# A graph layer with a gated delta-rule recurrence: norms by roots on ScalarE, logits with nodes stationary, five gate tiles behind the recurrence, output tile by tile

## The reference

```python
xn = layernorm(x)
x = x + gnn(xn, W, b, edges) + linear_attention(xn)
x = x + ffn(layernorm(x))

def ffn(h):                                   # E, TOPK, H, DK, DV, D = 4, 2, 8, 64, 64, 512
    scores = softmax(h @ Wgate);  rw, sel = top_k(scores, 2);  rw /= rw.sum()
    q = l2norm(silu(h @ Wq));  k = l2norm(silu(h @ Wk));  v = silu(h @ Wv)     # per head
    beta = sigmoid(h @ Wb);    g = -exp(A_log) * softplus(h @ Wa + dt_bias)
    # for each expert, over the nodes that chose it, in order:
    S = S * exp(g_t);  delta = (v_t - k_t @ S) * beta_t;  S += outer(k_t, delta);  o_t = (q_t / 8) @ S
    core = sum over the two chosen experts of rw * o
    core = core * rsqrt(mean(core * core, per head) + 1e-5) * o_norm_weight * silu(h @ Wg)
    return core @ Wo

def l2norm(x): return x * rsqrt(sum(x * x) + 1e-6)
```

## Time and profile before

| | us |
|---|---|
| median of 3 runs (lowest to highest) | 957.79 (955.58 to 961.64) |
| the profiled execution | 954.94 |
| its span, first to last instruction | 953.1 |
| PE busy in the span | 869.4 (91%) |
| DVE, ACT, POOL busy | 636.9, 258.9, 386.7 |
| chain that ended last, by engine | PE 55%, DVE 25%, POOL 10%, issue 6% |

### The profile page before, as it was taken

One profiled execution on the slowest core, in us unless ns is written; L12 is line 12 of the kernel. 1 busy time (PEld: TensorE's weight loads), 2 busy tenths in 40 slices (PEclk: granted clock), 3 DMA queues, 4 the chain that ended last, 5 costly groups with the idle time before them and its releaser, 6 DMA issues.

```text
span 953.1 us, 24758 instructions
## 1 busy us (share of the span) xinstructions
PE 869.4 (91%) x10668; PEld 561.1 (59%) x10668; DVE 636.9 (67%) x1308; ACT 258.9 (27%) x462; POOL 386.7 (41%) x313
## 2 busy tenths in 40 slices
PE   3989999999999899999999967899999999998598
PEld 2444443445666444444444447888899899887343
DVE  7999999968887323223436446777777687774284
ACT  1221113201222000015113114444344444443331
POOL 6221100001111300000589837776677777661572
PEclk9999999999999899999999989999999999999989
DMA  9500000120000330000036754444445444521452
GB/s 242 162 0 1 1 1 1 44 65 1 1 1 2 104 139 0 1 0 1 4 84 264 284 190 112 108 131 121 123 118 135 112 131 117 128 67 40 122 152 67
DMA packets 74964, 80.54 MB, mean 84 GB/s; under 512 B 34452, under 2 KB 57670, under 8 KB 74853
## 3 DMA queue, kind: packets, MB, share of 16 engines
q1 hardware_dynamic: 69733, 57.78, 22.2%
q0 software_dynamic: 5120, 21.14, 6.2%
HBM read 54.44 MB, written 24.39 MB: 83 GB/s over the span
## 4 chain that ended last, share of the span: by engine, by line
PE 55%; DVE 25%; POOL 10%; issue 6%; DMA 2%; ACT 1%; SPq 1%; DVEq 0%; POOLq 0%
PE bank L765 9%; PE bank L834 8%; PE bank L859 5%; PE bank L568 4%; PE bank L1022 4%; DVE rows L1490 3%; PE bank L554 3%; POOL nrm L1320 3%; DVE rows L1492 3%; PE bank L756 3%; POOL qkv_slots L1325 3%; DVE rows L1619 2%; DVE tB L1878 2%; PE bank L850 2%; POOL gb_slots L1315 2%
## 5 line engine op out<-in xcount | busy, mean ns | idle before, releaser
L756 PE MATMUL bank<-W,xT 128*128 128x512 f32 x296 | 128.3, 593 | 0.0
L756 PEld LDWEIGHTS bank<-W,xT 128*128 128x128 f32 x296 | 56.0, 190 | 69.9 <-issue 69.7
L765 PE MATMUL bank<-hs,big 125*125 125x512 f32 x200 | 86.6, 593 | 0.0
L1301 POOL TENSOR_TENSOR big<-big,ident_sb 125x125 f32<-125x125 f32 x10 | 11.4, 1142 | 173.8 <-ACT big L1085 173.8
L532 PE MATMUL bank<-W,xT 128*125 128x512 f32 x160 | 77.9, 600 | 0.0
L765 PEld LDWEIGHTS bank<-hs,big 125*125 125x125 f32 x200 | 37.3, 188 | 47.7 <-issue 47.5
L554 PEld LDWEIGHTS bank<-rows 128*126 128x126 f16 x360 | 43.5, 135 | 34.7 <-issue 24.2
L1625 DVE TENSOR_SCALAR rows<-iota_sb,tC 128x625 f16<-128x625 f16 x180 | 56.2, 378 | 10.5 <-PE bank L554 10.5
L554 PE MATMUL bank<-rows 128*126 128x313 f16 x360 | 58.9, 299 | 4.2 <-DVE rows L1625 4.1
L834 PE MATMUL bank<-big 64*64 64x64 f32 x1600 | 56.7, 218 | 1.9 <-issue 1.1
L1490 DVE TENSOR_SCALAR rows<-iota_sb,gbp 125x180 f16<-125x180 f16 x160 | 56.3, 352 | 0.0
(11 more groups left out here) (328 smaller groups left out, 1980.6 us busy)
## 6 DMA issues: line engine op xcount, KB each, us to landing
big<-qkv_slots SPq DMA_DIRECT2D x40, 256.0 KB, 3.4
rows<-step_rows SPq DMA_DIRECT2D x40, 128.0 KB, 3.1
rows<-gam_rows SPq DMA_DIRECT2D x40, 128.0 KB, 3.4
big<-qkv_slots SPq DMA_DIRECT2D x80, 64.0 KB, 2.7
big<-qkv_slots SPq DMA_DIRECT2D x40, 128.0 KB, 3.0
o_slots<-big SPq DMA_DIRECT2D x40, 128.0 KB, 2.8
x_all<-in_x SPq DMA_DIRECT2D x10, 224.0 KB
out<-tC SPq DMA_DIRECT2D x10, 224.0 KB
```

The costliest lines, as they stand in the source:

```text
L756: last = mm(bank[:, b0, :], xT[:, k, t * P:t * P + 128], W[:, w, k, :], start=(k == 0), stop=(k == KC - 1))
L765: last = mm(bank[0:P, t % 2, :], cnt[:, s, t * P:(t + 1) * P], hs[:, s, :], start=(s == 0), stop=(s == NT - 1))
```

## The change

Four edits in one.

1. Logits: `logit_rows`, `keep_logits` and the transposes go. `token_logits(t, k)` takes a tile of nodes as the stationary operand and the 20 columns of `wsm` as the moving one, so the logits come out with nodes in rows, in bank 5. The 40 products stand between the wide ones: 16 in the aggregation of tiles 8 and 9, 8 each in the projections (0,2), (1,0) and (1,1), which for tile 1 now come ahead of the last logits. The projection (0,3) goes to bank 5 and waits until VectorE has read the logits.
2. Norms of q and k: POOL's powers go. ScalarE takes the root (`row_norms`) after the Silu of the tile, for tiles 0 and 1 ahead of tile 2's Silu, and VectorE the reciprocal at the head of `unit_rows`.
3. `LATE = 5`: five gate tiles are done after the recurrence (`late_gate`, in four banks); their inputs are kept in `gbp`, which is free once the decays are done (`scal_done`), rather than in `kvbd`.
4. Output: one tile at a time. ScalarE takes the root (`root`), VectorE the reciprocal (in `finish`); POOL gathers only; TensorE transposes tile t + 1 and then does the product of tile t. ScalarE's Silu of the last two gate tiles stands between the first tiles' weighing.

The core of the diff:

```diff
-LATE = 7
+LATE = 5
...
-        lateT = [kvbd[:, :, :].rearrange("p c n -> p (c n)"), iota[:, :].bitcast(f32)] + [xT[:, k, LATE * P:N] for k in (2, 3)]
+        lateT = [gbp[:, :, :].rearrange("p c n -> p (c n)"), iota[:, :].bitcast(f32)] + [xT[:, k, LATE * P:N] for k in (2, 3)]
...
+            def token_logits(t, k):
+                n = E + 2 * H
+                pe.wait_ge(S["xT_done"], NT + t + 1)
+                return mm(bank[0:P, 5, t * n:(t + 1) * n], xT[:, k, t * P:(t + 1) * P], wsm[:, k, :], start=(k == 0), stop=(k == KC - 1))
+
+            def project_rows(t, w, tiles=()):
...
                 for k in range(KC):
                     last = mm(bank[:, b0, :], xT[:, k, t * P:t * P + 128], W[:, w, k, :], start=(k == 0), stop=(k == KC - 1))
-                last.then_inc(S["f_psum"], 1)
-
+                    if k == KC - 1:
+                        last.then_inc(S["f_psum"], 1)
+                    if tiles:
+                        for i in range(2):
+                            small = token_logits(tiles[k // 2], k % 2 * 2 + i)
+                if NT - 1 in tiles:
+                    small.then_inc(S["logit_psum"], 1)
...
                     last = mm(bank[0:P, t % 2, :], cnt[:, s, t * P:(t + 1) * P], hs[:, s, :], start=(s == 0), stop=(s == NT - 1))
+                    if t >= 8 and 1 <= s < 9:
+                        token_logits(2 * (t - 8) + (s - 1) // KC, (s - 1) % KC)
...
-            project_rows(0, 2)
+            project_rows(0, 2, (4, 5))
...
             for t in (8, 9):
                 transpose_row(1, t)
...
-            for w in range(3):
-                project_rows(1, w)
+            project_rows(1, 0, (6, 7))
+            project_rows(1, 1, (8, 9))
+            project_rows(1, 2)
             pe.wait_ge(W_loaded[3], 32)
+            pe.wait_ge(S["gate_exp"], 1)
             project_rows(0, 3)
...
-            for g in range(NT // 2):
-                for t in (2 * g, 2 * g + 1):
-                    gated_columns(t)
-                for t in (2 * g, 2 * g + 1):
-                    out_rows(t)
+            gated_columns(0)
+            for t in range(NT):
+                if t + 1 < NT:
+                    gated_columns(t + 1)
+                out_rows(t)
...
+            def row_norms(t):
+                act.wait_ge(S["ss_done"], t + 1)
+                A(nrm[:, t % 4, :], nrm[:, t % 4, :], ACT.Sqrt).then_inc(S["rn_done"], 1)
...
             feature_rows(0, 3)
+            for t in range(2):
+                row_norms(t)
             for t in range(2, NT):
                 for w in range(3):
                     feature_rows(t, w)
+                row_norms(t)
...
+            def root(t):
+                act.wait_ge(S["f_ms"], t + 1)
+                A(nrm[0:P, t % 4, 0:H], nrm[0:P, t % 4, 0:H], ACT.Sqrt).then_inc(S["rooted"], 1)
...
+            for t in range(LATE, LATE + 3):
+                late_gate(t)
+            for t in range(2):
+                weigh(t)
+            for t in range(2):
+                square(t)
+            late_gate(LATE + 3)
+            weigh(2)
+            late_gate(LATE + 4)
+            for t in range(NT):
+                root(t)
+                if t + 2 < NT:
+                    square(t + 2)
+                if t + 3 < NT:
+                    weigh(t + 3)
+                keep_columns(t)
...
-            inverse_norm(0)
             for t in range(NT):
-                if t + 1 < NT:
-                    inverse_norm(t + 1)
                 rows_out(t)
...
                 dve.wait_ge(S["rn_done"], t + 1)
+                step(V.reciprocal(nrm[:, b, :], nrm[:, b, :]))
...
             def finish(t):
-                dve.wait_ge(S["f_rs"], t // 2 + 1)
+                dve.wait_ge(S["rooted"], t + 1)
+                step(V.reciprocal(nrm[0:P, t % 4, 0:H], nrm[0:P, t % 4, 0:H]))
...
+            for t in range(NT):
+                moments(t)
+                if t + 2 < NT:
+                    mix_rows(t + 2)
+                finish(t)
+                if t in (1, 2, 3):
+                    gate_rows(LATE + 1 + t)
+                if t >= 2:
+                    last_sum(dve, V, t - 2)
```

More of the change, by code:

```diff
@@ L1228, in _, with late_gate @@
             keep_o(NCK - 1)
[L1230 removed]
+            def late_gate(t):
                 act.wait_ge(S["f_psum"], feature_count(t, 3))
[L1232 removed]
+                A(hs[:, t, :].rearrange("p (b j e) -> p b j e", b=2, e=DH), by_halves((t - LATE) % 4, P), ACT.Silu).then_inc(S["f_act"], 1)
             def weigh(t):
```

102 lines of the change are left out of this document (18 added, 84 removed).

## The result

The changed kernel takes **976.3 us** (median of 4 runs, 974.95 to 978.47) beside 956.68 us (4 runs, 954.83 to 961.64) for the kernel before: a ratio of 1.0194 (95% interval 1.0163 to 1.0224), 19.6 us slower, above the range of the prediction (949 to 970). The profiled execution took 974.99 us (span 973.2), against 954.94.

A forecast was written before the change was run, and what follows sets the result against it. The prediction took TensorE and POOL as nearly full in the feature stage, POOL's late scatters ending it, and TensorE as bounding the output stage. 957.79 + 3.4 (start) + 1.0 (output) gave 962.2 us, range 949 to 970.

The forecast's parts named there:

- Logits: Feature stage: 40 small products at 0.235 us replace 11.3 us of TensorE work; positions and gates 0.6 us later.
- The first hold: Feature stage, tile 3: TensorE stands 6.2 us for tile 2's Silu behind the first roots, plus 2.5 us slow clock.
- the second wait: Feature stage: VectorE waits for gates scattered and loaded back, delaying tile 4's squares and a root; nothing to 1.2 us.
- the 561.5 of the forecast: Predicted time of the recurrence's first transpose, +3.4 us (0 to +5.5) against the kernel before.
- The rival's 553.2: Recurrence start under the rival "the relief arrives", -4.9 us; chance 0.17.
- The recurrence itself is untouched: Recurrence: the prediction gave it no change in time.
- Output stage: After the recurrence: tile-by-tile output ends -0.8 to +1.3 us against before; +1.0 taken.
- the 10.43 us of the earlier trace: Behind the recurrence: TensorE's wait for the first gated tile, in which two more gate tiles take 6.9 us.
- The sum: Whole kernel: 3.4 us at the recurrence's start plus 1.0 in the output stage, +4.4 us.
- the relief arrives: Rival, feature stage: TensorE is not held at tile 3; recurrence starts 4.9 us earlier, 952.1 us in all; chance 0.17.

The follow-up runs named there:

- e8: The changed kernel with no row scatter issued until the gates are loaded back, GAMMA_AT still 2: 962.51 us, ratio 1.0058.
- e9: The changed kernel with the roots of tiles 0 to 5 later in ScalarE's order, GAMMA_AT left at 2: 968.47 us, ratio 1.0093.
- e1: The changed kernel with GAMMA_AT = 5 for 2, so VectorE reads the gates back after tile 5's rows: 965.82 us, ratio 1.0058.
- e7: The changed kernel with both GAMMA_AT = 5 and the roots of tiles 0 to 5 later on ScalarE: 955.25 us, ratio 0.998.
- e11: The changed kernel with the roots of tiles 0 to 5 later and row scatters waiting for the gates load: 957.73 us, ratio 0.9993.
- e16: The changed kernel with 16 small unused products added on TensorE ahead of the recurrence: 970.86 us, ratio 1.0128.
- e17: e11 with 16 small unused products added on TensorE ahead of the recurrence: 949.29 us, ratio 0.9915.
- e2: The changed kernel with 98 small unused products added on TensorE ahead of the recurrence: 976.52 us, ratio 1.0176.
- e10: The kernel before with only the changed output stage, three late gate tiles kept: 955.75 us, ratio 0.9982.
- e4: The kernel before with 30 small unused products added on TensorE ahead of the recurrence: 961.16 us, ratio 1.0003.
- e18: e11 with 82 small unused products added on TensorE ahead of the recurrence: 950.77 us, ratio 0.9911.

## Why the prediction was wrong

**Logits: right.** Predicted 0.235 us a small product and gates 0.6 us later (-4 to +3). Measured: a pair of products adds 1.30 - 0.86 = 0.44 us to the pitch of the wide one, 0.22 each; the logits are read at 441.62 for the predicted 443.0, and the first gate scatter starts at 459.67 against 460.42, 0.75 us earlier.

**The first hold: right in its mechanism, a little too large.** Predicted a stand of 6.2 us and 2.5 us of slow clock, which put tile 3 8.5 us late; measured a stand of 4.29 (5.98 in e8, where tile 2 ran at a granted clock of 1.00) with the clock at 0.65 behind it, and 6.8 us by e9. ScalarE was idle for 8.87 us ahead of the first Sqrt, where the prediction asked for some 10. The root took 0.216 us and the reciprocal 0.244, for 0.25 and 0.3; in the steady part of the stage both are hidden, as said.

**The step that failed** is the price of the second wait. The prediction's sentence reads "A second wait of VectorE, for gates that are scattered until 486.5 and loaded back behind that", priced at nothing to 1.2 us with 8 us for landing and load. It cost 13.2 us by e1 and 13.1 by e8. The wait was seen, with its place and with what is queued behind it; the price was taken from transfers as they ran in the kernel before. But the same edit takes POOL's powers away, which had kept the row scatters off until 492.50, and so lets six of them out beside the load. It landed up to 14.2 us after its issue, for 4. The rest of the sentence holds: in e8, where the load lands after 3.7 to 4.2 us, the second wait does not hold TensorE, and the start, 557.62, is even 3.9 us ahead of the 561.5 of the forecast. The prediction asked what the faster POOL makes possible, and not with what the earlier scatters collide.

The rival's 553.2 without any hold (e7 and e11 measured 552.71 and 551.55) plus the measured 6.8 and 13.2 is 573.2, against 572.75. As the two holds were measured against that same 572.75, this shows only that they add up and that nothing else of size is in the start.

**"The recurrence itself is untouched": wrong in the time, by 5.3 us in the two profiles.** Its code is, but not its place in TensorE's instruction stream. Moving the place back takes 5 to 8 us off in e16 and e17 and nothing that shows in e2, on top of a variation of some 5 us between executions; how much of the 5.3 us is the change's stays open.

**Output stage: +1.0 predicted, +0.13 in the two profiles, +0.7 over all of them** (65.8 against 65.1), inside its bounds. The first tile is finished 20.4 us after the last output copy, as the prediction has it (905.5, 20.3 after), but the parts are others than it says: by e10's one profile the tile-by-tile form alone gains 1.5, and the two more gate tiles, which were to fit into the 10.43 us of the earlier trace rows without a price, cost some 2.3 at the first root.

**The sum** was +4.4 (3.4 and 1.0), for +20.05 between the two profiled executions. The rival "the relief arrives" had the start without holds right to 0.5 us (e7) and 1.7 us (e11), and was given 0.17. No rival held that the relief of POOL slows the transfer on which the next root depends.

## What to carry to other kernels

An engine that gets faster releases its transfers earlier and closer together: for each one, look at what is loaded at that moment and who waits for it, and price that load by a trace in which such transfers run beside it. An operation that waits for another engine is best put behind everything in its own engine's order that does not depend on it (two lines of order were worth 20 us here). And where a long dense stretch follows an edit, compare its length before and after even if its code is the same; a handful of idle instructions ahead of it can help to tell whether its place is the cause (here it did in one group of runs and not in another).

## What the runs showed of the hardware that was not expected

- TensorE stalls by 0.2 to 1.8 us at places that fit a grid of 256 instructions in its stream; all idle put down to issue is 8 to 18 us in a recurrence of some 330. Adding 128 records (256 instructions) leaves the places where they were, adding 30 or 98 moves them to other groups, as counted. The queue of instructions in the profile moves 87 packets with 1.43 MB, 16.4 KB each. The Trainium skill (Runtime: NRT & Kernel Launch, "Instruction fetch mechanics") says that an engine's instruction memory is refilled in blocks of 16 KiB, 256 instructions, and that crossing into the next costs little and is mostly hidden. The traces agree on the block; that it is hidden does not hold for this loop.
- The sum of the stalls depends in part on where they fall: with the loop at +30, where they fall mostly in float16 products of 64x64 (16 in 0.4 us), it is 10.4 to 18.2 us; elsewhere, where they fall mostly in f32 products, it is 8.2 to 12.6 us, but 15.6 in e2. Moving them made the kernel 5 to 8 us shorter in e16 and e17. In one group of runs (e2 to e4) this difference did not show in the times, on a chip where it did later (e16 to e18); this was not explained.
- Two loads of 160 KB land 3.6 to 4.2 us after their issue alone, 8.9 and 14.2 us with six scatters of 786 KB beside them, and 7.0 and 21.7 us (e1) or 8.0 and 25.5 us (e7) with ten or more.
